# Fourth layer, attention over the batch: another order of VectorE's score and value products and of ScalarE's squares and exponentials

## The reference, cut to what matters

```
q = _dora_linear(xn, mag_q, dir_q, A_q, B_q, bias_q)   # x @ W.T + b, W scaled by its norm
k = xn @ k_w.T + k_b
v = _dora_linear(xn, mag_v, dir_v, A_v, B_v, bias_v)
attn = softmax(q k^T / 4)     # per position and head: 8 x 8
s = (attn v) @ out_w.T + out_b
```

## Time and profile before

| what | value |
|---|---|
| median of three runs | 4565.76 us |
| the profiled execution's own time | 4563.96 us |
| its span, first to last instruction | 4562.2 us |
| TensorE busy in the span | 4382.1 us (96%) |
| VectorE busy | 2499.0 us (55%) |
| ScalarE busy | 1683.8 us (37%) |
| mean granted TensorE clock | 0.981 of full |

### The profile page before, as it was taken

One profiled execution on the slowest core, in us unless ns is written; L12 is line 12 of the kernel. 1 busy time (PEld: TensorE's weight loads), 2 busy tenths in 40 slices (PEclk: granted clock), 3 DMA queues, 4 the chain that ended last, 5 costly groups with the idle time before them and its releaser, 6 DMA issues. The chain is left out here.

```text
span 4562.2 us, 56266 instructions
## 1 busy us (share of the span) xinstructions
PE 4382.1 (96%) x19737; PEld 2563.8 (56%) x19737; DVE 2499.0 (55%) x5815; ACT 1683.8 (37%) x3241; POOL 201.5 (4%) x324
## 2 busy tenths in 40 slices
PE   7999989999999999999999999999998798999999
PEld 3444446766666666666766666666656454333333
DVE  6666653252523325242342533878788787666665
ACT  3444442232232323223232323444433221455555
POOL 0222200000000000000000000000000000000000
PEclk9999999999999999999999999999999899999999
DMA  3011011111121211212111121000000000111110
GB/s 85 14 19 36 16 47 74 74 66 65 56 93 65 79 60 65 83 56 93 65 64 75 65 84 52 1 1 1 1 1 1 20 1 1 34 20 23 25 24 21
DMA packets 51059, 196.47 MB, mean 43 GB/s; under 512 B 9672, under 2 KB 19280, under 8 KB 33624
## 3 DMA queue, kind: packets, MB, share of 16 engines
q1 hardware_dynamic: 49984, 192.84, 12.8%
q10 hardware_dynamic: 816, 0.20, 0.0%
HBM read 169.54 MB, written 4.33 MB: 38 GB/s over the span
## 5 line engine op out<-in xcount | busy, mean ns | idle before, releaser
L1104 PE MATMUL l_exp_out<-l_w,l_hidden 128*128 128x256 f32 x4096 | 905.3, 381 | 0.3
L1094 PE MATMUL l_hid<-l_xn_t,l_w 128*128 128x512 f32 x2048 | 891.1, 593 | 0.0
L1104 PEld LDWEIGHTS l_exp_out<-l_w,l_hidden 128*128 128x128 f32 x4096 | 774.1, 190 | 118.9 <-issue 9.0
L1218 ACT ACTIVATE l_hidden<-l_hid,l_w 128x512 f32<-128x512 f32 x512 | 351.5, 686 | 930.7 <-PE l_hid L1094 930.7
L1094 PEld LDWEIGHTS l_hid<-l_xn_t,l_w 128*128 128x128 f32 x2048 | 388.9, 190 | 466.4 <-issue 453.6
L488 DVE TENSOR_REDUCE l3f_row_max<-l3f_bank 128x1 f32<-128x512 f32 x512 | 327.7, 685 | 177.6 <-PE l3f_bank L368 177.2
L1385 DVE SCALAR_TENSOR_TENSOR l_moe<-l_exp_out,l_gates,l_moe 128x256 f32<-128x256 f32 x256 | 123.6, 483 | 449.9 <-PE l_exp_out L1104 444.2
L444 ACT ACTIVATE l3f_prob_t<-l3f_bank 128x512 f32<-128x512 f32 x512 | 277.3, 596 | 217.8 <-PE l3f_bank L375 217.6
L485 DVE CUSTOM_DVE_ANT_0 l_masked<-l_bank,l_mask 128x256 f32<-128x256 f32 (+3 forms) x512 | 226.6, 487 | 157.0 <-PE l_bank L368 156.1
L375 PE MATMUL l3f_bank<-l3f_qk_t 32*128 32x512 f32 x1024 | 303.0, 637 | 0.9 <-ACT l3f_prob_t L444 0.5
L368 PE MATMUL l3f_bank<-l3f_qk_t 32*128 32x512 f32 x1024 | 297.2, 644 | 5.5 <-DMA l3f_qk_t<-l3f_packed 5.2
(11 more groups left out here) (458 smaller groups left out, 6086.8 us busy)
## 6 DMA issues: line engine op xcount, KB each, us to landing
l_w<-in_w SPq DMA_DIRECT2D x128, 1024.0 KB, 4.9
l_mix<-l_cum SPq DMA_DIRECT2D x32, 512.0 KB, 3.8
l_qk_t<-l_packed SPq DMA_DIRECT2D x128, 64.0 KB
l3f_qk_t<-l3f_packed SPq DMA_DIRECT2D x128, 64.0 KB
all_x<-in_x SPq DMA_DIRECT2D x8, 512.0 KB, 6.4
out_x<-all_x SPq DMA_DIRECT2D x7, 512.0 KB, 3.0
l_hidden<-in_fp4w SPq DMA_DIRECT2D x1, 2304.0 KB
l_qk_t<-l_max_rows SPq DMA_DIRECT2D x128, 2.0 KB
```

The lines of the kernel that those rows point to most:

```text
L1094: ins = nc.tensor.matmul(bank[:, :], w1[:, e % 2, c, f * P:(f + 1) * P], xn_t[:, c, :], start=c == 0, stop=c == CT - 1)
L1104: ins = nc.tensor.matmul(bank[:, 0:C], hidden[:, e % 2, f, j * P:(j + 1) * P], w2[:, e % 2, f, :], start=f == 0, stop=f == HF - 1)
L1218: hid.empty(nc.scalar.activation(hidden[:, e % 2, f, :], bank[:, :], ACT.Relu, bias=w[:, B1][:, e * HF + f:e * HF + f + 1]), (e, f))
```

## The change

No instruction is added or taken away. Instructions move inside the lists of VectorE and ScalarE; TensorE's list is the same. There are four moves:

1. Slot -1: VectorE takes both halves of quad 0's score products before it moves v out, where the second half came behind v.
2. The first half of quad 1's score products goes from the start of slot 0 to slot -1, between `normalise(1)` and `squares_out(0, 0)`.
3. Slots 1, 3 and 5: v banks 0 and 1 are moved out between the first and the second value product, where they came behind both, and the second half of the score products goes ahead of v banks 2 and 3.
4. All odd slots: ScalarE squares guide banks 4 to 7 ahead of the exponential, where it came behind.

```diff
@@ ScalarE, the loop over slots
                 if odd:
                     squares_in(j, range(0, HALF))
+                if odd:
+                    squares_in(j, range(HALF, B))
                 if scores:
                     act.wait_ge(centred, u + 2)
                     nc.scalar.activation(prob[...], prob[...], ACT.Exp, scale=float(D) ** -0.5).then_inc(exp_ready, 1)
...
-                if odd:
-                    squares_in(j, range(HALF, B))
@@ VectorE, the loop over slots
-                if next_scores:
+                if next_scores and u:
                     scores(u + 1, 0)
                 if next_values:
                     values(u, 0)
+                if odd:
+                    if u < 0:
+                        scores(u + 1, 1)
+                    value_in(j, (0, 1))
+                if next_values:
                     values(u, 1)
-                if odd:
-                    value_in(j, (0, 1))
                 if 0 <= u - 1:
                     output_in(u - 1, 0)
...
                     output_in(u - 1, 1)
+                if next_scores and u >= 0:
+                    scores(u + 1, 1)
                 if odd:
                     value_in(j, (2, 3))
-                if next_scores:
-                    scores(u + 1, 1)
                 if next_values:
                     values(u, 2)
                     values(u, 3)
...
                     if j + 1 < TJ:
                         normalise(j + 1)
+                    if u < 0:
+                        scores(u + 2, 0)
                     squares_out(j, 0)
```

## The result

Four runs of the changed kernel gave 4526.71 to 4537.47 us, median 4530.77; the kernel before stands at 4565.6 (4559.97 to 4570.94, four runs). The ratio is 0.9922, with a 95% interval of 0.991 to 0.9934. The forecast was 4537.8 with a range of 4531.0 to 4546.0. The profiled execution took 4534.40 us, 29.6 less than the one before.

What follows compares the result with a forecast made beforehand. TensorE was taken to bound the program, with an alternating VectorE-TensorE chain in slots -1 and 0 and VectorE in slots 6 to 8. 12.0 + 5.9 + 5.8 + 4.2 = 27.9 us, so 4565.76 - 28 = 4537.8 us, range 4531 to 4546.

Steps and rivals of the forecast that it cites:

- Slots -1 and 0: First two slots: an alternating VectorE-TensorE chain shortens, TensorE's second score sums of slot 0 moving from 3621.54 to 3609.5, 12.0 us.
- Slots 1, 3, 5: Odd slots: three TensorE stops go, and in slots 1 and 3 the clock's fall too; 5.9, 5.8 and 4.2 us.
- Together 4.23 us: Odd slots: the summed idle of TensorE's three stops in slot 1, 1.29, 1.95 and 0.99 us, all expected to go.
- stop (a): Slot 1: TensorE's 1.29 us wait before the second output product, whose bank holds v bank 0, expected to go.
- (b): Slot 1: TensorE's 1.95 us wait before the second score sums, expected to go.
- (c): Slot 1: TensorE's 0.99 us wait before the transposes for a guide bank not yet squared, expected to go.
- The clock's part: Slots 1 and 3: without stops the granted clock stays full, giving 1.7 and 1.6 us back.
- my bound for slots -1 and 0 alone: First two slots: all lost time returns, at most 19 us, 7 more than counted; 35 us in total.
- a clock that keeps what the stops gave: Rival, odd slots and slot 0: clock falls remain, gain only 21 us, time 4544.6 us; chance 0.14.
- a new wait in the odd slots: Rival, odd slots: a new wait replaces the old, only slots -1 and 0 pay, 12 us, 4553.8; chance 0.07.
- nothing: Rival: TensorE loses its gain again before slot 6, less than 9 us, about 4563; chance 0.03.
- slower: Rival: new stops keep TensorE at its lower clock level; 60 us of that gives 4598 us; chance 0.02.

Runs made afterwards that it cites:

- act_only: Kernel before with ScalarE's move alone: guide banks 4 to 7 squared ahead of the exponential; ratio 0.9965, median 4550.05 us.
- first_only: Kernel before with only VectorE's moves of slots -1 and 0 (moves 1 and 2); ratio 0.9966, median 4552.77 us.
- norm_early: Changed kernel with block 1's inverses and normalising ahead of quad 0's second score half in slot -1; ratio 0.9926, median 4535.55 us.
- odd_only: Kernel before with only VectorE's moves of slots 1, 3 and 5 (move 3); ratio 0.9983, median 4562.56 us.
- before_p1: Kernel before, unedited, profiled once more; stage began at 3545.6 us and took 336.4 us, last stage 687.9 us.

## Why the prediction was right, and where it was wrong

Three steps of it failed, and the second is the largest: the cost of a stop in the odd slots was put too low, the next stage was taken to move with the changed one and keep its length, and the range was given no width for the runs ("Runs of this kernel differ by some 5 us at most").

**Slots -1 and 0**: 12.0 forecast, 12.1 measured (91.94 to 79.85 us from the stage's start to slot 1). Each link stood within 0.3 us: second score half at 3576.04 (3576.01), VectorE at the first sum of squares at 3590.69 (3590.97), exponential over at 3595.4 (3595.4), second sums at 3609.42 (3609.5). The clock did not fall behind the four stops that are left there, 1.20, 1.92, 1.27 and 0.84 us, which I had left open.

**Slots 1, 3, 5**: 5.9, 5.8 and 4.2 forecast, 6.6, 6.6 and 4.9 measured; slots 2 and 4 are 0.2 longer, which I had at nothing. Slot 1 is 35.7 us, a little under the 36 to 37 that I gave as a sign. The step that was mis-sized is "Together 4.23 us": I took the idle time in the rows as what a stop costs. By TensorE's start times, stop (a) held the way from the first output product to the first score sums at 5.08 us, now 3.55: 1.53 for 1.29 of idle. Before the change:

```profile
3642.00 1.89 PE L2321 MATMUL l3a_bank<-l3a_w,l3a_att_t 128*128 128x256 f32 x8
3645.18 1.97 PE L2321 MATMUL l3a_bank<-l3a_w,l3a_att_t 128*128 128x256 f32 x8 [1.29 <-DVE l3a_v L2560]
3647.08 1.92 PE L2284 MATMUL l3a_bank<-l3a_score_prod,l3a_blocks 128*32 128x512 f32 x16
```

The missing 0.24 us is in these rows: the two groups of output products took 1.89 and 1.97 us on either side of the stop, and 3.62 together without it, since they then overlap. With (b), 5.55 us from value sums to score sums and now 3.52, it is 2.03 for 1.95, and with (c), 4.82 from guide banks to transposes and now 3.66, 1.16 for 0.99: the sum is 4.7. The clock's part, 1.7 and 1.6, came as said (7.27 to 5.63 us in slot 1). VectorE kept up, with waits of 0.2, 0.5, 0.3 and 0.9 against 0.4, 0.5, 0.3 and 1.1 by my count.

**The stage**: 27.9 forecast, 29.8 measured, 306.8 in all profiles. So 1.9 of the 6.9 us by which I missed are terms of the sum.

**The last stage**: "the next stage ... with it", that is, unchanged. This is the step that failed by most. The last stage is 4.0 us shorter in the mean of five profiles each, 3.6 of it in its first 80 us, where the clock was higher: 0.77 instead of 0.72 in the first 30 us, and no fall in the second 30 where four of five profiles of before had one. What decides at which clock the stage is entered stays open. Keeping TensorE busy there raised the clock and brought no gain in the program, so it is not shown to be a handle. The remaining 1 us is scatter ahead of the stage.

**The range** ended at 4531.0 by my bound for slots -1 and 0 alone. It had no width for the runs themselves: all 68 of the kernel before lie between 4559.8 and 4578.0, mean 4569.6, and the 12 of the changed kernel between 4526.0 and 4538.1, mean 4532.9. By these means the gain is 36.6 us. With such scatter it is luck on which side of 4531.0 a median of four runs falls; that the gain is larger than 27.9 is not.

**The rivals**: a clock that keeps what the stops gave, a new wait in the odd slots, nothing, slower: none came. The first had some truth in other kernels: in act_only, first_only, norm_early and odd_only the clock gave or took 1 to 9 us in places that the edit did not touch.

No version here beats the changed kernel by more than its runs differ; norm_early's stage is 0.6 us shorter.

## What to carry to other kernels

Follow the order of each engine by hand from the trace's own durations: where every link of a chain is a row, the sum came out within 0.1 us in 12. Cost a stop by the time from start to start of the bottleneck engine's instructions around it: here that was 0.1 to 0.2 us more than its idle time. And ask for what lies behind the changed stage as well: a program that is bound by TensorE can gain or lose several us there by the clock alone, so a part of a change must be judged on both: odd_only gave 14 us in its stage and 6 to 8 in the program, act_only 6 in its stage and some 16 in the program.

## What the runs showed of the hardware that was not expected

- The place of a clock fall inside this stage belongs to the program, not to the execution. In five profiles of the kernel before, with stages that began up to 6.3 us apart, the slots had the same lengths to 0.1 us, falls included, and so in five of the changed kernel. The granted clock shows it too. In before and before_p1, 42.5 us after the start of each one's stage (3540.9 and 3545.6):

```profile
3583.43:3590.26 6.83, 5.22 (x20) 1.90 (x21) 4.44 (x11) 0.60 (x1) 0.00 (x0) 0.50 0.00 0
3588.06:3594.89 6.83, 5.20 (x20) 1.87 (x21) 4.46 (x11) 0.60 (x1) 0.00 (x0) 0.50 0.00 0
```

  In all nineteen profiles of all the kernels here, with stages that began between 3533.4 and 3546.1 us, the lower level that stands at the stage's start began 1.8 to 2.0 us ahead of it. What ties the two together is not shown. The Trainium skill, TensorE: Matmul & The Clock Gate, "What you observe", has the point at which the clock rises vary by some 500 ns from run to run. This trace does not agree inside this stage. In the last stage what varied was whether a fall came at all: the second 30 us of before had 0.89 of the upper level four times and 1.00 once.
- The same stop of 1.95 us before the same sums had three outcomes in one program: the sums took 3.22 us in slot 1, 2.58 in slot 3 and 1.92 in slot 5 of the kernel before. Another edit far ahead exchanged the slots (first_only). The granted clock from these sums on was 0.77, 0.76 and 1.00 of the upper of its two levels, 2.4 GHz.
- The last stage took 683.7 to 698.5 us with the same instructions, the kernels with added products left out. Between profiles of one program it differed by up to 9.7 us.
